# Segment sums with each tile's weight matrix in two column parts

## What is computed

```
h   = max(layernorm(x), 0)                      # 12500 x 16
m   = (h[src] @ W_node.T + edge_attr @ W_review.T) * edge_w
out = x + segment_sum(m, dst, 12500)            # all f32
```

## Time and profile before

| what | value |
|---|---|
| median of 3 runs | 1766.9 us (1765.85 to 1771.57) |
| the profiled execution's own time | 1771.62 us |
| its span, first to last instruction | 1769.5 us |
| TensorE matmul / weight load busy | 1544.8 / 1524.7 us |
| VectorE, ScalarE, GpSimd busy | 1455.6, 970.8, 1247.3 us |
| mean granted TensorE clock | 0.942 of full speed |

### The profile page before, as it was taken

The page is one execution under the profiler, slowest core; times in us unless marked ns, Lnnn a source line. Parts: engine busy times, 40 slices in busy tenths (PEclk is TensorE's granted clock), DMA queues, the critical chain, the costliest instruction groups (busy, mean ns, idle before and its releaser), DMA issues.

```text
span 1769.5 us, 75737 instructions
## 1 busy us (share of the span) xinstructions
PE 1544.8 (87%) x25040; PEld 1524.7 (86%) x25040; DVE 1455.6 (82%) x3393; ACT 970.8 (55%) x4245; POOL 1247.3 (70%) x1177
## 2 busy tenths in 40 slices
PE   0119998999989899999989998998989998999977
PEld 0019998999989899999989898998989898999975
DVE  7998887888888787888888787878878887878864
ACT  1114364665656564756656564756656564756653
POOL 2287777777777777777777777777777777777400
PEclk9659999999999999999999999999999999999965
DMA  3524345454545445454444454454545454554443
GB/s 116 92 36 113 100 114 114 110 122 103 125 106 128 112 114 127 104 129 109 118 113 111 116 120 116 118 125 105 118 110 114 115 125 109 122 130 100 119 86 48
DMA packets 513913, 195.34 MB, mean 110 GB/s; under 512 B 475071, under 2 KB 496196, under 8 KB 513212
## 3 DMA queue, kind: packets, MB, share of 16 engines
q1 hardware_dynamic: 474853, 178.88, 39.9%
q0 software_dynamic: 36000, 9.29, 5.9%
q10 hardware_dynamic: 2609, 1.55, 0.5%
HBM read 186.67 MB, written 2.92 MB: 107 GB/s over the span
## 4 chain that ended last, share of the span: by engine, by line
PE 46%; DVE 24%; issue 12%; DVEq 8%; POOL 6%; ACT 2%; DMA 1%; ACTq 0%; POOLq 0%; SPq 0%
PE found L1110 26%; PE seg L1143 11%; POOL vals_p L530 6%; DVE big L770 5%; PE seg L1134 5%; DVEq L875 4%; PE edge_h L1124 3%; DVE masked L824 3%; DVEq L867 2%; DVE perm L860 2%; DVE masked L838 1%; DVE mid L845 1%; ACT mid L592 1%; DVE by_rank L715 1%; DVE by_rank L714 1%
## 5 line engine op out<-in xcount | busy, mean ns | idle before, releaser
L530 POOL DMA_INDIRECT vals_p<-h_ext,idx_t x1125 | 1228.7, 1092 | 350.9 <-issue 330.6
L1110 PE MATMUL found<-table,big 128*128 128x112 f16 (+2 forms) x16384 | 870.6, 215 | 57.8 <-DVE by_rank L888 32.3
L1110 PEld LDWEIGHTS found<-table,big 128*128 128x128 f16 x16384 | 846.1, 100 | 63.9 <-DVE by_rank L888 34.9
L592 ACT ACTIVATE sel_p<-hit_p,wgt_t 128x64 f32<-128x64 f16 x1125 | 292.8, 335 | 429.2 <-DVE hit_p L845 416.2
L592 ACT ACTIVATE mid<-mid,wgt_t 128x64 f32<-128x64 f16 x2000 | 500.1, 333 | 36.8 <-DVE mid L845 34.9
L1143 PE MATMUL seg<-mid 128*96 128x64 f32 x4000 | 400.4, 256 | 15.9 <-ACT mid L612 11.3
L1143 PEld LDWEIGHTS seg<-mid 128*96 128x96 f32 x4000 | 379.3, 173 | 18.0 <-ACT mid L592 11.8
L770 DVE TENSOR_SCALAR big<-low_all,own 128x2004 f16<-128x2004 f16 x516 | 361.2, 742 | 2.8 <-DMA low_all<-low_dram 2.8
L879 DVE SCALAR_TENSOR_TENSOR acc<-seg,count_s,acc 96x64 f32 x400 | 112.2, 280 | 168.5 <-issue 126.8
L1134 PE MATMUL seg<-sel_p,vals_p 128*80 128x64 f32 x2250 | 201.8, 237 | 6.9 <-DMA vals_p<-h_ext,idx_t 6.9
L1134 PEld LDWEIGHTS seg<-sel_p,vals_p 128*80 128x80 f32 x2250 | 183.3, 154 | 7.8 <-DMA vals_p<-h_ext,idx_t 3.8
(11 more groups left out here) (131 smaller groups left out, 546.1 us busy)
## 6 DMA issues: line engine op xcount, KB each, us to landing
low_all<-low_dram SPq DMA_DIRECT2D x128, 501.0 KB
mid<-in_edge_attr_dram SPq DMA_DIRECT2D x400, 160.0 KB
vals_p<-in_edge_attr_dram SPq DMA_DIRECT2D x232, 160.0 KB
vals_p<-h_ext,idx_t POOLq DMA_INDIRECT x1125
big<-in_dst_dram SPq DMA_DIRECT2D x1, 1562.5 KB
big<-in_edge_weight_dram SPq DMA_DIRECT2D x1, 1562.5 KB
h_ext<-mid SPq DMA_DIRECT2D x2, 781.2 KB
low_all<-low_dram ACTq DMA_DIRECT2D x2, 501.0 KB
```

Source lines behind the costliest of these rows:

```text
L530: pool.indirect_dma_start(vals_p[:, q % RP, j, R:F], None, h_ext, bass.IndirectOffsetOnAxis(ap=idx_t[:, q * J + j:q * J + j + 1], axis=0), ...
L592: last = nc.scalar.activation(sel[:, j, :], hit[:, j, :], ACT.Copy, scale=wgt_t[:, bass.ds(tile + j, 1)])
L1110: last = nc.tensor.matmul(found[x % 2][:, r * P:r * P + n], hot[:, x // 2 % 2, a, col:col + P], rows, start=(a == 0 and part == 0), stop=( ...
```

## The change

In both sums each matmul of a tile becomes two. The first takes the 64 edge features (weight columns 0 to 63) and writes PSUM partitions 0 to 63; the second takes the columns of h (64 to 79 in `sum_p`, 64 to 95 in `sum_s`) and writes the partitions of the same numbers. Both stream the same `sel`. The two products of a tile follow each other, then come those of the next tile; the increment is on the last of the ten. Nothing else is changed.

```diff
--- before.py
+++ after.py
@@ -1125,14 +1125,19 @@
                                                 by_rank[:, :, :, g * J + q].rearrange("p i f -> p (i f)"), start=True, stop=True)
                     last.then_inc(unsorted, 1)
 
+
+                parts_p = ((0, 64), (64, 80))
+                parts_s = ((0, 64), (64, 96))
+
                 def sum_p(q, turn_of_slot, x):
                     pe.wait_ge(sel_p_in, ps * NQ + q + 1)
                     slot = slot_of(x)
                     pe.wait_ge(ea_p[slot], ps * (loads_of(slot) * 16) + turn_of_slot * 16 + 16)
                     pe.wait_ge(h_in[slot], ps * (groups_of(slot) * J * 16) + turn_of_slot * (J * 16) + J * 16)
                     for j in range(J):
-                        last = nc.tensor.matmul(seg_p(x), vals_p[:, slot, j, :], sel_p[:, slot_of(x), j, :],
-                                                start=(j == 0), stop=(j == J - 1))
+                        for low, high in parts_p:
+                            last = nc.tensor.matmul(seg_p(x)[low:high, :], vals_p[:, slot, j, low:high], sel_p[:, slot_of(x), j, :],
+                                                    start=(j == 0), stop=(j == J - 1))
                     last.then_inc(summed_p, 1)
 
                 def sum_s(u, g):
@@ -1140,8 +1145,9 @@
                     pe.wait_ge(ea_s[g % RS], ps * (NSG // RS * 16) + u * (GROUPS // RS * 16) + (g // RS * 16 + 16))
                     pe.wait_ge(h_placed, ps * NSG + u * GROUPS + g + 1)
                     for j in range(J):
-                        last = nc.tensor.matmul(seg_s(g), vals_s[:, g % RS, j, :], sel_s[:, g % RS, j, :],
-                                                start=(j == 0), stop=(j == J - 1))
+                        for low, high in parts_s:
+                            last = nc.tensor.matmul(seg_s(g)[low:high, :], vals_s[:, g % RS, j, low:high], sel_s[:, g % RS, j, :],
+                                                    start=(j == 0), stop=(j == J - 1))
                     last.then_inc(summed_s, 1)
 
                 def bank_free(before, x, last):
```

## The result

The change makes the kernel slower by 57.5%: 2787.8 us (2784.4 to 2788.8) against 1769.2, ratio 1.5752, 95% interval 1.5724 to 1.5781. That is 1019 us, where 32 us less was forecast, and outside the range of 1718 to 2000.

What follows compares the result with a forecast made beforehand. It took TensorE to bound the kernel, GpSimd's gathers next and VectorE close behind. -25 us in the loop and -7 in the last phase, off a median of 1766.9, gave 1735 us; range 1718 to 2000 (forecast alone 1720 to 1755).

Steps and rivals of the forecast that it cites:

- the load sets the pace of a pass: Both sums on TensorE: passes start 73 or 86 ns apart because of their 80 or 96 weight columns, 0.8 ns a column.
- f32 streams take 54 to 55 ns of 64 columns: Both sums: streaming 64 f32 columns of sel takes 55 ns at 2.4 GHz, twice that at 1.2.
- column positions run side by side: Both sums: the two parts of a tile load and stream together, as in L1195, so a pair takes 60 ns.
- Rival C: Both sums: TensorE empties at every change of size, +2606 us, 4370; shorter emptying between 2000 and that; chance 0.20.
- The rule set beside C: Both sums: the skill says changing tiling mode drains the engine, 64 and 32 wide being two modes; left open, no size.
- A: Rival, both sums: the second part streams only after the first, 114 ns a pair, +212 us, 1979; chance 0.12.
- B: Rival, both sums: streams overlap but loads follow one another, +31 to +62 us, 1813; chance 0.08.
- D: Rival, loop: pairs take 60 ns but VectorE is the true bound, so no change, 1765; chance 0.08.
- The second half of the sum: Gain if parts overlap: -25 us in the loop, after an allowance for VectorE, and -7 in the last phase, together -32.
- the last phase: 1696 to 1750 us, clock halved: at least 50 of 160 ns a pass saved, a third of 20 us, -7.
- The bound named for the loop: GpSimd's gathers, at 1.374 us each, limit the loop's gain to 31.9 us, with VectorE close behind.
- The load at the slow clock: Last phase at 1.2 GHz: 160 ns a pass for 96 columns, 107 for 64, against the skill's clock-independent rate.

Runs made afterwards that it cites:

- f2: Changed kernel with the second part widened to 40 columns, so both tiles are 64 wide (some columns land elsewhere or are computed twice): 1758.2 us, ratio 0.9938 to kernel before.
- f1: Changed kernel with three parts of one width, 32 columns (last of p tiles 16), at positions 0, 32, 64: 1762.7 us, ratio 0.9959 to kernel before.
- h1: Kernel before with GpSimd's gathers cut from five to four a group from the eighth group on: 1763.7 us, ratio 0.9970.
- h2: Three parts of one width as in f1, plus gathers cut from five to four a group: 1736.8 us, ratio 0.9823 to kernel before.
- f3: Changed kernel with its two loops exchanged, a group's five 64-column products first, then its five narrow ones: 2139.8 us, ratio 1.2089 to kernel before.
- f4: Changed kernel with only sum_p split, in 64 and 16, sum_s as before: 2155.1 us, ratio 1.2169 to kernel before.
- e runs: First runs of the kernels of f1, f2, f3 and f4, on a chip where the kernel before took 2695 us: 2914, 2681, 3049 and 3075 us.
- e3: Same kernel as f3, the change with its loops exchanged, on a chip where the kernel before took 2695 us: 3049 us.
- g1: Same kernel as h1, kernel before with four gathers a group, on a chip where the kernel before took 2756 us: 2424 us.
- g2: Same kernel as h2, three parts of one width and four gathers, on a chip where the kernel before took 2756 us: 2634 us.

## Why the prediction was wrong, point by point

- **That the load sets the pace of a pass, and that f32 streams take 54 to 55 ns of 64 columns**: right. f2 and f1 run at just those numbers once loads are out of the way.
- **That column positions run side by side**: right for one width, and that is all that the earlier trace rows showed. The step that failed is "I take 60, since the nearest row, L1195, shows column positions side by side": four tiles of one size were read as evidence for two of different sizes. A pass-and-its-partner costs 244 ns in the s groups and 237 in the p groups (half of 488 and of 474), not 60.
- **Rival C** was what happened, at a chance of 0.20, and its price was too high by a factor of 2.6 in the added time (2606 against 1019). It emptied the engine at every pass; in fact the two passes of an f32 call stay together, so the width changes once a call, and an emptying costs 95 ns and an open load, not a whole record. (244-86) x 4000 + (237-73) x 2250 = 1001. The lower bound of C, "between 2000 and that", was right. The range left C out, and with it the 0.20.
- The rule set beside C in the prediction: the Trainium skill (TensorEngine Tiling, Key Properties) has it that a change of tiling mode, not of tile, drains TensorE. Here the trace and the runs agree: 95 ns without a start at each change of width, none at a change of position with the same width (f1, f2), and 0.11 us more at the entry from 128-column products. I gave it 0.20 because no row showed it; but no row spoke against it either, and the rows said nothing about mixed widths. An open rule against the change deserved more than a row that bears on another case.
- **A** named one part of the price, streams one after the other, but without the emptying and the open loads. **B** and **D** played no part.
- **The second half of the sum**, -25 in the loop and -7 in the last phase for products that do overlap, can be read off f1 and f2: they give 7 and 12 where I had 32. The bound named for the loop (the gathers) is right, by h1 and h2, and VectorE behind it fits the waits. Mis-sized was "They then run from 296.3 at 1.374 us": they ran at 1.406, and TensorE's last p sum came 3 us earlier in place of 31.9. The last phase, from TensorE's turn of the ranks (L1118) to the end, went from 82.4 (1687.06 to 1769.5) to 77.6 us (1682.16 to 1759.8): 5 against 7. That this is near is luck. TensorE's busy time up to L1195 fell there by 16 us (52.4 to 36.7), in part because its granted clock rose from 0.55 to 0.68, and its waits for VectorE's adds (L879) grew from 4.6 to 11.8 us; the sum had neither.
- **The load at the slow clock**, 160 ns for 96 columns: right, as far as the runs show. In the slow part of the kernel after (granted clock 0.50) the two matmuls of a 64-column product start 162 ns apart and those of a 32-column one 109, against 107 and 80 at full clock: 32 columns more cost 53 ns in place of 27, twice as much. And f2's pairs take (2.39-1.30)/10 = 109 ns at that clock, the 107 to 110 of the prediction. The rate of columns / 1.2 ns that the Trainium skill states (TensorE: Matmul & The Clock Gate, LDWEIGHTS) fits at 2.4 GHz (80 ns for 96 columns, with a pass of 86) and not at 1.2, where a pass takes 160. The section names no clock; that it holds at either was my reading.

## What to carry to other kernels

Column tiles of one width at different positions run side by side, and splitting a wide f32 operand so can beat its weight load; tiles of two widths in turn cost 120 to 130 ns at each change, more than the two streams of the product itself (108 ns). Before costing such a split, write down the width of each product in order, those of the neighbours too, and count the changes; if widths must differ, order by width. And where three engines are within a few per cent of each other, a saving on one of them is not worth its sum: 89 us of TensorE's busy time gave 7.

## What the runs showed of the hardware that I had not expected

- The emptying at a change of width: 95 to 98 ns after the last stream's end, with the next load in the open behind it; at the entry from f16 products of 128 columns 0.11 us more than before.
- The length of a gather on GpSimd depends on what VectorE does meanwhile, it seems: the mean is 970 ns in the kernel after (VectorE 52% busy), 1040 in f3 (69%), 1060 in f4 (68%), 1092 before (82%) and 1113 in f1 (83%), with a median of 947 in the last two. On the chip of the e runs it is 1019 ns at 48% (e3), so the share alone doesn't set it. In the kernel before the gathers longer than 1.6 us overlap VectorE's L860, L845 or L842 in three of four cases, the shorter ones in 18 to 31 of 100. That is a coincidence in time and not a test; what makes them long was not tried.
- On some chips this program is slower by half: the kernel before took 2695 and 2756 us there, with holes of some 0.5 us before single instructions of TensorE. A fifth of the gathers less gave 12% there (g1, 2424 us), against 0.3% elsewhere (h1); with f1's three parts too (g2, 2634 us) it gave 4.5%. Why is open.
